# Last stage of a decoder layer: gate and up products with the weights stationary and the tokens moving, the tile loop written out

## The chip, the core and the metric

The kernel runs as one launch on one core of a Trainium2 chip. The metric is the device time of the launch in microseconds. A core has five engines that run their own instruction streams and wait for each other through semaphores: PE (TensorE, matmuls), DVE (VectorE), ACT (ScalarE), POOL (GpSimd) and SP (SyncE, which here issues loads). A PE matmul has a stationary operand, which a weight load (PEld in the profile) puts into the array, and a moving operand that streams through it.

## What is computed

A decoder layer on x of shape 4 x 256 x 256 (1024 tokens of width 256): causal attention with 16 heads, a first gated feed-forward network whose four experts are picked by token id, and a second one whose expert is the best of four by a router. After each part stands x = layernorm(x + part). The change is in the second network. The reference computes it for all experts and selects:

```python
x = tokens of width 256
probs = softmax(x @ Wr + br)
top_w, top_idx = top_k(probs, 1)
g = einsum('td,edf->tef', x, Wg)        # 4 experts, F = 1024
u = einsum('td,edf->tef', x, Wu)
h = silu(g) * u
y = einsum('tef,efd->ted', h, Wd)
out = y[top_idx] * top_w
```

## The kernel before

**Tiles.** The tokens are sorted by expert through a scratch tensor in memory, so that each of NS = 11 tiles of P = 128 tokens needs one expert only (1024 tokens fill 8, and 3 more leave room for the part-filled tiles at the ends of the experts). For each tile the PE computes gate and up (128 tokens x 1024 columns each, contracted over D = 256, NK = 2 steps of 128) and the down product (128 x 256, contracted over F = 1024, NF = 8 steps).

**Three products for one.** Every operand is kept as the sum of two fp16 numbers, hi and lo. A product is hi·hi + hi·lo + lo·hi, so three matmuls (helper `three`, L1286 to L1290). The weights of all experts lie in the tensors wf_hi and wf_lo, EW = 6144 columns an expert, in the order gate, up, down. They are split into hi and lo on the way in: ACT makes hi (`split_hi`, L554), DVE makes lo (`split_lo`, L799), 1024 columns a step. Eight of these steps fall into the last stage: `ENDING` puts 2 ahead of tile 0 and 2 into each of the tiles 0, 1 and 2.

**One tile, before.** PE transposes the tile's tokens (`x_T3`), so that features lie on the partitions; ACT and DVE split the result into a_hi and a_lo (`x_hi3` L736, `x_lo3` L1195). `gate_up` multiplies with a_hi and a_lo **stationary** and 512 weight columns **moving**. It runs in two halves of the F columns, gate and up of a half in two PSUM banks (0, 1 and 2, 3), 12 matmuls a half. ACT applies silu to gate (`silu`, L742), DVE multiplies by up (`gated`, L1202) into hh (128 tokens x 1024, fp32). As tokens lie on the partitions of hh, PE has to transpose it: `h_T3` (L1654), 8 fp32 transposes into the banks 4 and 5. ACT and DVE split the transposed h (`h_hi3` L749, `h_lo3` L1209, 1024 columns each), and `down` multiplies with h stationary and 256 columns of the down weights moving, 24 matmuls into bank 7. Then come residual and layernorm (`statistics`, L1217 to L1223, and `finish`, L1228, on DVE, with two small operations on POOL, L531 and L533, between them), and POOL scatters the rows to the output (L535).

**Order.** Each engine runs the tiles in the order of its code. In tile i PE does gate_up half 0 of tile i, h_T3 of tile i-1, x_T3 of tile i+1, gate_up half 1 of tile i, down of tile i-1. Down of the tiles 0 and 1 is held back until all weights are split (down(0) after tile 2, down(1) within tile 3). Gate_up half 0 of a tile waits until both halves of the tile before are through `gated` (semaphore h3). Four tiles are written out (`PEEL`), six run in a hardware loop of two tiles a turn, and the last stands behind it with a short way out: 8 transposes (L1708), 5 matmuls that only keep the array busy (L1296), and the last down (L1719).

**Addresses.** The expert of a tile is known only at run time. PE loads its number into a register (`expert_of`, TENSOR_LOAD, L1626) and computes the address of each moving weight slice from it. These register operations stand in PE's instruction stream between the matmuls and run on its sequencer: one that makes several sums (FUSED_REGOPS in the profile, ISA in the listings below) and one with a single sum (ALU_OP, or REGISTER_ALU) to every three matmuls.

Of the kernel before, what the change touches and what calls it, by code (L numbers as in the profile page):

```python
# [12 lines left out]
F32, F16, BF16, I32 = mybir.dt.float32, mybir.dt.float16, mybir.dt.bfloat16, mybir.dt.int32  # L13
ALU, ACT, AX = mybir.AluOpType, mybir.ActivationFunctionType, mybir.AxisListType

P = 128
# [34 lines left out]
PEEL = 4  # L51
LOOPS = (NS - 1 - PEEL) // 2
assert PEEL + 2 * LOOPS + 1 == NS
# [8 lines left out]
WARM_START, WARM_GAP, WARM_END = 30, 8, 5  # L62
# [3 lines left out]
def build(nc, x_tok, xT, ids, wqkvT, woT, ctxT, Wr, br, Wf, out):  # L66
    ctx = ExitStack()
    with ctx:
# [7 lines left out]
        wf_hi = sb("wf_hi", [P, E * EW], F16)  # L76
        wf_lo = sb("wf_lo", [P, E * EW], F16)
# [120 lines left out]
        xrow = carve([D], F32)  # L198
# [3 lines left out]
        def h_of(i):  # L202
            return (first_hi[i], first_lo[i]) if isinstance(i, int) and i < 2 else (h_hi, h_lo)
# [3 lines left out]
        def ps16(k, rows=slice(0, P)):  # L207
# [29 lines left out]
        ld3 = [sem(f"ld3_{i}") for i in range(PEEL + 2)]  # L237
# [8 lines left out]
        endT, end_hi, end_lo = sem("endT"), sem("end_hi"), sem("end_lo")  # L246
        a3T, a3hi, a3lo, gu_a, gu_b, sg3, h3, h3T, h3hi, h3lo, y3, r3, bn3, mv3, ve3, xrow_rdy, rs3, f3 = (
            sem(n) for n in ("a3T", "a3hi", "a3lo", "gu_a", "gu_b", "sg3", "h3", "h3T", "h3hi", "h3lo", "y3",
                             "r3", "bn3", "mv3", "ve3", "xrow_rdy", "rs3", "f3"))
# [87 lines left out]
        def _(sp):  # L337
# [64 lines left out]
            for i in range(NS):  # L402
                row = sp.value_load(row_i[0:1, i:i + 1], min_val=0, max_val=NR3 - P)
                if i == 0:
                    sp.wait_ge(scat3, 16 * NS)
                sp.dma_start(XS[:, i, :], sorted3[bass.ds(row, P), :]).then_inc(ld3[min(i, PEEL + 1)], 16)

# [138 lines left out]
        def _(act):  # L546
# [179 lines left out]
            def x_row(i):  # L726

                act.wait_ge(a3T, i)
                a.activation(xrow, XS[:, bass.ds(i, 1), 0:D].rearrange("p o d -> p (o d)"),
                             ACT.Copy).then_inc(xrow_rdy, 1)  # L730

            def x_hi3(i, p):
                act.wait_ge(a3T, i + 1)
                if not (isinstance(i, int) and i < 2):
                    act.wait_ge(gu_b, i - 1)
                a.activation(a_hi[p], ps[:, 6, 0:D].rearrange("p (k t) -> p k t", k=NK), ACT.Copy).then_inc(a3hi, 1)  # L736

            def silu(i, half):
                act.wait_ge((gu_a, gu_b)[half], i + 1)
                if not (isinstance(i, int) and i < 1):  # L740
# [4 lines left out]
            def h_hi3(i):  # L745
                act.wait_ge(h3T, i + 1)
                if not (isinstance(i, int) and i < 3):
                    act.wait_ge(y3, i)
                a.activation(h_of(i)[0], ps[:, 4:6, :].rearrange("p c (k t) -> p (c k) t", t=P),  # L749
                             ACT.Copy).then_inc(h3hi, 1)  # L750

            def tile(i, p, first=False, last=False, splits=((), ())):
                if not isinstance(i, int):
                    x_row(i + 1)
                silu(i, 0)
                if not first:
                    h_hi3(i - 1)
                if not last:
                    x_hi3(i + 1, 1 - p)
                for c in splits[0]:  # L760
                    split_hi(c)
                silu(i, 1)
                for c in splits[1]:
                    split_hi(c)

            x_hi3(0, 0)
# [3 lines left out]
            for i in range(PEEL):  # L770
                splits = ENDING[i + 1] if i + 1 < len(ENDING) else (0, 0)
                tile(i, i % 2, first=i == 0, splits=[range(n, n + splits[0]), range(n + splits[0], n + sum(splits))])
                n += sum(splits)
            assert n == NCH
            act.wait_ge(ld3[PEEL + 1], 16 * (NS - PEEL - 1))
# [983 lines left out]
```

## Time and profile before

| | |
|---|---|
| Runs | 316.97, 317.5 and 321.75 us; median 317.5 us |
| The profiled execution | span 317.3 us |
| PE busy | 249.7 us (79%), 2015 matmuls |
| PE weight loads | 168.8 us (53%) |
| DVE busy | 192.4 us (61%) |
| ACT busy | 134.8 us (42%) |
| POOL busy | 66.7 us (21%) |
| Mean granted TensorE clock | 0.940 |

The last stage, which the change touches, runs from 195.6 us, when the first gate product starts, to the end. A row of the profile gives the source line, the engine, the operation, what it writes and reads, and a count. Busy time of PE is drawn with modelled ends, so the distance between the starts of matmuls says more than their duration: a burst of n equal matmuls that takes t, where one lasts d, has a distance of (t - d)/(n - 1).

### The profile page before, as it was taken

Reading aid. Unit: us, or ns where it says so; the run is one execution under the profiler, and the core shown is the slowest. Engines: PE = TensorE matmul, PEld = TensorE weight load, DVE = VectorE, ACT = ScalarE, POOL = GpSimd, SP = SyncE. Lnnn points to the kernel's source line nnn. Section 1 sums busy time; section 2 is a strip of 40 time slices with the busy share of each in tenths; the row PEclk is TensorE's granted clock in tenths of the full one; section 3 lists DMA queues with packets and bytes.
Section 4 is the critical chain, followed back from the end, with each engine's and each line's share of the span. In section 5 each row is a group of like instructions: output and inputs, shape, how many; then the busy total and the mean of one; then the engine's idle time right before and its main releaser. Section 6 shows DMA issues by size and latency. Waiting matters only on the chain.

```text
span 317.3 us, 5932 instructions
## 1 busy us (share of the span) xinstructions
PE 249.7 (79%) x2015; PEld 168.8 (53%) x2032; DVE 192.4 (61%) x415; ACT 134.8 (42%) x225; POOL 66.7 (21%) x128
## 2 busy tenths in 40 slices
PE   3776589879989775798785566776969999999990
PEld 3454466656756543485665423433745666666570
DVE  4865677777896656868568437566344445545441
ACT  4450555764949744554424332455212312333210
POOL 8400000100140532210113860000203211122222
PEclk9797899999999999979899579999899999999997
DMA  6999045222252445104067123300000000000000
GB/s 213 334 311 276 3 152 181 69 70 66 69 166 69 115 153 153 44 22 135 1 247 284 44 83 89 105 0 0 2 17 20 0 13 17 17 17 17 9 10 6
DMA packets 17416, 28.51 MB, mean 90 GB/s; under 512 B 2733, under 2 KB 12974, under 8 KB 17392
## 3 DMA queue, kind: packets, MB, share of 16 engines
q1 hardware_dynamic: 16048, 25.28, 25.9%
q0 software_dynamic: 1344, 2.90, 2.6%
q8 instruction: 16, 0.26, 0.3%
q14 instruction: 8, 0.07, 0.1%
HBM read 19.43 MB, written 9.50 MB: 91 GB/s over the span
## 4 chain that ended last, share of the span: by engine, by line
PE 56%; DVE 21%; issue 8%; ACT 6%; DMA 3%; POOL 3%; SPq 1%; POOLq 0%; ACTq 0%; DVEq 0%
PE ps L1290 34%; PE ps L1654 3%; DVE arena L965 3%; DVE wf_lo L799 2%; PE ps L1361 2%; PE ps L1400 2%; PE ps L1603 2%; ACT wf_hi L554 2%; PE ps L1548 2%; DVE arena L960 1%; PE ps L1357 1%; DMA ring<-wqkvT 1%; DVE arena L1167 1%; POOL sorted L514 1%; DVE arena L939 1%
## 5 line engine op out<-in xcount | busy, mean ns | idle before, releaser
L1290 PE MATMUL ps<-wf_hi,arena 128*128 x336 | 84.0, 333 | 10.6 <-DVE arena L1202 3.4
L1290 PE MATMUL ps<-wf_lo,arena 128*128 x168 | 55.9, 333 | 0.0
L1290 PEld LDWEIGHTS ps<-wf_hi,arena 128*128 128x128 f16 x336 | 33.4, 99 | 36.1 <-issue 16.1
L742 ACT ACTIVATE arena<-ps 128x512 f32<-128x512 f32 x22 | 13.1, 597 | 68.9 <-PE ps L1290 68.9
L1202 DVE SCALAR_TENSOR_TENSOR arena<-ps,arena 128x512 f32<-128x512 f32 x22 | 15.2, 691 | 22.4 <-PE ps L1654 12.3
L799 DVE SCALAR_TENSOR_TENSOR wf_lo<-ring,wf_hi 128x1024 f16<-128x1024 f32 x17 | 20.6, 1219 | 12.6 <-ACT wf_hi L554 7.5
L1290 PE MATMUL ps<-xT_hi,arena 128*128 (+1 forms) x88 | 21.4, 307 | 1.1 <-DVE arena L1135 1.1
L1290 PEld LDWEIGHTS ps<-wf_lo,arena 128*128 128x128 f16 x168 | 16.7, 99 | 9.4
L531 POOL TENSOR_SCALAR veps<-mv 128x1 f32<-128x1 f32 x11 | 2.5, 225 | 87.3 <-DVE mv L1223 87.3
L965 DVE TENSOR_REDUCE arena<-ps 128x4 f16<-128x1024 f32 x16 | 19.6, 1223 | 1.1 <-PE ps L1361 1.1
L1290 PE MATMUL ps<-arena,xT_hi 128*128 128x512 f16 (+1 forms) x64 | 16.5, 347 | 3.0 <-DVE arena L920 2.1
L554 ACT ACTIVATE wf_hi<-ring 128x1024 f16<-128x1024 f32 x17 | 17.7, 1052 | 0.1
L1217 DVE SCALAR_TENSOR_TENSOR arena<-ps,arena 128x256 f32<-128x256 f32 x11 | 5.3, 483 | 19.6 <-PE ps L1290 17.4
L601 ACT ACTIVATE arena<-ps 128x1024 f32<-128x1024 f32 x16 | 16.5, 1033 | 1.1 <-PE ps L1384 0.7
L960 DVE TENSOR_REDUCE arena<-ps 128x4 f16<-128x512 f32 x16 | 11.0, 689 | 8.6 <-PE ps L1361 8.4
L1357 PE MATMUL ps<-maskS,identB 128*128 128x512 bf16 x27 | 11.0, 408 | 5.1 <-DVE arena L965 3.9
L1361 PE MATMUL ps<-arena 128*128 128x128 f16 x144 | 13.4, 232 | 2.0 <-DVE wf_hi L946 0.9
L535 POOL DMA_INDIRECT out<-arena,out_i x11 | 12.0, 1091 | 13.9 <-DVE arena L1228 13.9
L1400 PE MATMUL ps<-arena 128*32 128x256 f32 (+1 forms) x256 | 13.7, 331 | 1.2 <-ACT arena L607 1.1
L1209 DVE TENSOR_TENSOR arena<-ps,arena 128x1024 f16<-128x1024 f32 x10 | 12.2, 1225 | 3.2 <-ACT arena L749 3.2
L584 ACT ACTIVATE arena<-ps 64x1024 f16<-64x1024 f16 x6 | 6.1, 1018 | 18.1 <-PE ps L1326 18.1
L1548 PE MATMUL ps<-identF,arena 128*128 128x128 f32 x22 | 5.3, 328 | 10.6 <-DVE arena L1172 10.6
(227 smaller groups left out, 534.4 us busy)
## 6 DMA issues: line engine op xcount, KB each, us to landing
ring<-Wf SPq DMA_DIRECT2D x17, 512.0 KB, 3.8
sorted<-fill SPq DMA_DIRECT2D x1, 4515.0 KB, 20.6
arena<-Wf SPq DMA_DIRECT2D x7, 512.0 KB, 8.3
arena<-sorted SPq DMA_DIRECT2D x20, 129.0 KB, 2.2
sorted<-fill SPq DMA_DIRECT2D x1, 1161.0 KB, 6.1
ring<-xT SPq DMA_DIRECT2D x4, 256.0 KB, 5.1
X<-x_tok SPq DMA_DIRECT2D x1, 1024.0 KB, 7.5
ring<-ctxT SPq DMA_DIRECT2D x2, 512.0 KB, 4.1
```

What stands on the lines that cost most here:

```text
L554: a.activation(chunk_dst(ORDER[n], True), src, ACT.Copy, scale=W_SCALE).then_inc(c_hi, 1)
L601: a.activation(Pf[n % 2][:, 1:3], ps[:, 4:6, :], ACT.Exp, scale=DK ** -0.5).then_inc(exped, 1)
L742: a.activation(sg[:, half * 512:(half + 1) * 512], ps[:, 2 * half, :], ACT.Silu, scale=1 / W_SCALE).then_inc(sg3, 1)
L799: v.scalar_tensor_tensor(out=chunk_dst(ORDER[n], False), in0=staged(n)[0], scalar=W_SCALE, in1=chunk_dst(ORDER[n], True), op0=ALU.mult, op ...
L960: v.tensor_reduce(dst[:, 0], ps[:, 0, :].rearrange("p (a k) -> p a k", a=G), AX.X, ALU.max, negate=True).then_inc(maxed, 1)
L965: v.tensor_reduce(dst[:, 1], ps[:, 1:3, :].rearrange("p c (a k) -> p a c k", a=G), AX.XY, ALU.max, negate=True).then_inc(maxed, 1)
L1202: v.scalar_tensor_tensor(out=hh[:, half * 512:(half + 1) * 512], in0=ps[:, 2 * half + 1, :], scalar=inv, in1=sg[:, half * 512:(half + 1) * ...
L1209: v.tensor_tensor(lo, ps[:, 4:6, :].rearrange("p c (k t) -> p (c k) t", t=P), hi, ALU.subtract).then_inc(h3lo, 1)
L1290: last = t.matmul(dst, xs(k), ws(k), start=(k == 0 and m == 0), stop=(k == nk - 1 and m == 2))
L1357: t.matmul(ps[:, bank, :], identB[:, :], maskS[:, :, :].rearrange("p a k -> p (a k)"), start=True, stop=False)
L1361: last = t.matmul(ps[:, bank, i * P:(i + 1) * P], q[:, h, qt * P:(qt + 1) * P], k[:, h // 2, kt * P:(kt + 1) * P], start=not diag, stop=(n ...
L1400: last = t.matmul(ps[i * HEAD:(i + 1) * HEAD, 6, kt * P:S], Vs[:, TB * b + kt, at_:at_ + HEAD], q, start=kt == 0, stop=kt == TB - 1, tile_ ...
```

## The change

The three weight parts change their role only in gate and up. `gate_up` now takes 128 weight columns as the stationary operand and the 128 tokens (a_hi, a_lo) as the moving one. The result has F columns on the partitions and tokens in the free direction, which is what `down` needs, and so the transposes of h (L1654, L1708) and the banks 4 and 5 fall away. A tile's gate and up take 96 matmuls of 128 columns in place of 24 of 512. `h_hi3` and `h_lo3` read hh from SBUF, in two halves of 512 columns. Gate and up of a half signal apart, so silu may start after gate. Gate_up of a half now waits for the same half of the tile before. All eleven tiles are written out, each with its own load semaphore, with the `xrow` copy gone. The expert is loaded a tile ahead, behind `x_T3`, as a byte offset, and the addresses of three hi/lo weight pairs are made together by one register operation ahead of nine matmuls. The `WARM_END` matmuls are gone, `down` waits for r3 (residual read) in place of mv3 and for h3lo in halves.

```diff
-            def h_T3(i):
-                pe.wait_ge(h3, 2 * i + 2)
-                for k in range(NF):
-                    last = t.transpose(ps[:, 4 + k // 4, (k % 4) * P:(k % 4 + 1) * P], hh[:, k * P:(k + 1) * P],
-                                       identF[:, :])
-                last.then_inc(h3T, 1)
             def expert_of(i):
-                return pe.value_load(tile_i[0:1, 1, bass.ds(i, 1)], min_val=0, max_val=E - 1)
+                e = pe.value_load(tile_i[0:1, 1, i:i + 1], min_val=0, max_val=E - 1)
+                return pe.snap(e * (2 * EW))
+            def weights(base, at_, n):
+                cols = bass.ds(base + 2 * at_, 2 * n)
+                return wf_hi8[:, cols].bitcast(F16), wf_lo8[:, cols].bitcast(F16)
+            def addressed(pairs, stationary):
+                for w in pairs:
+                    for half in w:
+                        pe.lower_ap(half, for_matmul_weights=stationary)
-            def gate_up(p, half, expert):
+            def gate_up(i, half, base):
+                p = i % 2
+                if i >= 1:
+                    pe.wait_ge(h3, 2 * i + half - 1)
                 for n in range(2):
-                    at_ = lambda k, n=n: expert * EW + (n * NK + k) * F + half * 512
-                    last = three(ps[:, 2 * half + n, :], lambda k: a_hi[p][:, k], lambda k: a_lo[p][:, k],
-                                 lambda k: wf_hi[:, bass.ds(at_(k), 512)],
-                                 lambda k: wf_lo[:, bass.ds(at_(k), 512)], NK)
-                last.then_inc((gu_a, gu_b)[half], 1)
+                    ws = [weights(base, (n * NK + k) * F + (4 * half + c) * P, P) for c in range(4) for k in range(NK)]
+                    for j, (hi, lo) in enumerate(ws):
+                        c, k = divmod(j, NK)
+                        if j % 3 == 0:
+                            addressed(ws[j:j + 3], True)
+                        dst = ps[:, 2 * half + n, c * P:(c + 1) * P]
+                        t.matmul(dst, hi, a_hi[p][:, k], start=k == 0, stop=False)
+                        t.matmul(dst, hi, a_lo[p][:, k], start=False, stop=False)
+                        last = t.matmul(dst, lo, a_hi[p][:, k], start=False, stop=k == NK - 1)
+                    last.then_inc((gu_a, gu_b)[half], 1)
...
+            for i in range(NS):
+                pe.wait_ge(a3lo, i + 1)
+                gate_up(i, 0, bases[i])
+                if i + 1 < NS:
+                    x_T3(i + 1)
+                    bases.append(expert_of(i + 1))
+                if i == AHEAD3:
+                    down(1, bases[1])
+                gate_up(i, 1, bases[i])
+                if i == 2:
+                    down(0, bases[0])
+                elif i >= 3:
+                    down(i - 1, bases[i - 1])
+            down(NS - 1, bases[NS - 1])
```

ACT's order in a tile becomes silu(i, 0), x_hi3(i+1), split, h_hi3(i, 0), silu(i, 1), split, h_hi3(i, 1); DVE's becomes gated(i, 0), x_lo3(i+1), split, h_lo3(i, 0), gated(i, 1), split, h_lo3(i, 1), then statistics and finish of tile i-1.

The first place is PE in the middle of a tile, from the end of gate_up half 0 to the start of half 1. Before:

```order
L1290 MATMUL ps<-wf_hi,arena 128x512
L1650 REGISTER_ALU
L1654 MATMUL ps<-identF,arena 128x128 [waits h3lo,h3]
L1654 MATMUL ps<-identF,arena 128x128 x7
L1633 REGISTER_ALU
L1638 MATMUL ps<-identF,arena 128x128 [waits a3lo,xrow_rdy]
L1638 MATMUL ps<-identF,arena 128x128
L1290 ISA
L1290 MATMUL ps<-wf_hi,arena 128x512
L1290 REGISTER_ALU
L1290 MATMUL ps<-wf_lo,arena 128x512
```

The same place of the change:

```order
L1634 MATMUL ps<-arena,wf_lo 128x128
L1617 MATMUL ps<-identF,arena 128x128 [waits a3lo,ld3_9]
L1617 MATMUL ps<-identF,arena 128x128
L1599 TENSOR_LOAD tile_i
L1599 ISA x2
L1610 ISA [waits h3]
L1632 MATMUL ps<-arena,wf_hi 128x128
L1633 MATMUL ps<-arena,wf_hi 128x128
L1634 MATMUL ps<-arena,wf_lo 128x128
```

The eight transposes are gone, the load of the next expert has moved in, and one register operation now stands ahead of nine matmuls (the last three rows come three times before the next).

The second place is PE at the end of the program, from the last down but one. Before:

```order
L1290 MATMUL ps<-wf_hi,arena 128x256
L1708 MATMUL ps<-identF,arena 128x128 [waits h3lo,h3]
L1708 MATMUL ps<-identF,arena 128x128 x7
L1296 MATMUL ps<-wf_hi,ones 128x512 [waits a3lo]
L1296 MATMUL ps<-wf_hi,ones 128x512 x4
L1719 ISA [waits end_lo,mv3]
```

And of the change:

```order
L1650 MATMUL ps<-wf_lo,arena 128x256
L1651 MATMUL ps<-wf_hi,arena 128x256
L1610 ISA [waits h3lo,r3]
L1649 MATMUL ps<-wf_hi,arena 128x256
L1650 MATMUL ps<-wf_lo,arena 128x256
```

The last down now follows the one before it with only the wait for r3 and h3lo between them.

The third place is DVE around a tile in the steady part. Before:

```order
L1202 SCALAR_TENSOR_TENSOR arena<-ps,arena 128x512 [waits h3T,sg3]
L1209 TENSOR_TENSOR arena<-ps,arena 128x1024 [waits h3hi]
L1194 REGISTER_ALU
L1195 TENSOR_TENSOR arena<-ps,arena 128x256 [waits a3hi]
L1199 REGISTER_ALU
L1202 SCALAR_TENSOR_TENSOR arena<-ps,arena 128x512 [waits h3T,sg3]
```

And of the change:

```order
L1184 SCALAR_TENSOR_TENSOR arena<-ps,arena 128x512 [waits h3hi,h3lo,gu_a,sg3]
L1175 TENSOR_TENSOR arena<-ps,arena 128x256 [waits a3hi]
L1191 TENSOR_TENSOR arena<-arena 128x512 [waits h3hi]
L1184 SCALAR_TENSOR_TENSOR arena<-ps,arena 128x512 [waits h3hi,h3lo,gu_b,sg3]
L1191 TENSOR_TENSOR arena<-arena 128x512 [waits h3hi]
L1200 SCALAR_TENSOR_TENSOR arena<-ps,arena 128x256 [waits scat_out1,y3]
```

`gated` no longer waits for the transposes (h3T), and the split of h has become two operations of half the size that belong to the same tile.

## Rows read from the trace of the kernel before

**Rows 1.** Chain of work that ended last, tiles 0 to 2; start us, us, what

```profile
195.64 2.76 PE ps L1290 x12
...
198.62 2.60 PE ps L1290 x12
...
202.82 2.76 PE ps L1290 x12
...
219.13 1.24 DVE wf_lo L799
...
220.61 7.04 PE ps L1290 x36
```

**Rows 2.** The same chain, from the down product of tile 2 to the last

```profile
236.69 2.79 PE ps L1290 x24
...
239.69 2.76 PE ps L1290 x12
242.45 0.87 PE ps L1654 x8
...
243.54 5.21 PE ps L1290 x36
...
257.84 0.55 issue
...
286.04 2.76 PE ps L1290 x12
...
303.97 0.87 PE ps L1708 x8
304.84 1.08 PE ps L1296 x5
...
306.07 2.81 PE ps L1719 x24
```

**Rows 3.** Timeline of PE at 89 us; start us, us, engine, line, operation

```profile
89.24 0.61 PE L1361 MATMUL ps<-arena 128*128 128x128 f16 x8
```

**Rows 4.** Source L1361: duration in ns least, median, most; first and last start

```profile
L1361 PE MATMUL ps<-arena x144: 217/219/314, 21.2 to 94.8; 128*128 128x128 f16 x144
```

**Rows 5.** Timeline of PE at 205 us, fp32 transposes

```profile
205.41 1.04 PE L1654 MATMUL ps<-identF,arena 128*128 128x128 f32 x8
```

**Rows 6.** Source L1290, PE's sequencer, 264.6 us to 266.4 us

```profile
L1290 PEldq FUSED_REGOPS  x7: 46/46/46, 264.7 to 266.2; - x7
```

**Rows 7.** Source L1626, the load of the expert's number, 240 us to 290 us

```profile
L1626 PEldq FUSED_REGOPS  x14: 46/151/151, 242.7 to 285.4; - x14
L1626 PEldq TENSOR_LOAD <-tile_i x8: 299/303/312, 242.8 to 285.1; - x8
```

**Rows 8.** Groups by line, 195 to 309 us; busy us, mean ns, idle before

```profile
L1202 DVE SCALAR_TENSOR_TENSOR arena<-ps,arena 128x512 f32<-128x512 f32 x22 | 15.2, 691 | 22.4 <-PE ps L1654 12.3 <-ACT arena L742 10.2
L742 ACT ACTIVATE arena<-ps 128x512 f32<-128x512 f32 x22 | 13.1, 597 | 68.9 <-PE ps L1290 68.9
L1209 DVE TENSOR_TENSOR arena<-ps,arena 128x1024 f16<-128x1024 f32 x10 | 12.2, 1225 | 3.2 <-ACT arena L749 3.2
...
L799 DVE SCALAR_TENSOR_TENSOR wf_lo<-arena,wf_hi 128x1024 f16<-128x1024 f32 x7 | 8.5, 1221 | 0.5 <-ACT wf_hi L554 0.4
...
L1217 DVE SCALAR_TENSOR_TENSOR arena<-ps,arena 128x256 f32<-128x256 f32 x11 | 5.3, 483 | 19.6 <-PE ps L1290 17.4 <-PE ps L1719 2.2
L1195 DVE TENSOR_TENSOR arena<-ps,arena 128x256 f16<-128x256 f32 x11 | 4.6, 415 | 1.0 <-ACT arena L736 1.0
```

**Rows 9.** Stretches: busy of PE, PEld, DVE, ACT, POOL; granted clock; DMA share

```profile
217.50:220.60 3.10, 0.02 (x1) 0.00 (x0) 2.82 (x3) 1.54 (x2) 0.00 (x0) 1.00 0.00 0
220.60:224.00 3.40, 3.39 (x19) 2.48 (x20) 0.00 (x0) 0.00 (x0) 0.00 (x0) 0.60 0.00 0
...
234.00:236.60 2.60, 0.00 (x0) 0.00 (x0) 1.75 (x5) 0.89 (x2) 0.06 (x1) 1.00 0.00 0
...
248.70:267.40 18.70, 18.12 (x117) 11.62 (x116) 9.01 (x18) 5.59 (x10) 3.77 (x6) 1.00 0.04 12
```

More of the change, by code:

```diff
@@ L236, in build @@
         ld2 = [sem(f"ld2_{i}") for i in range(NSA)]
[L237 removed]
+        ld3 = [sem(f"ld3_{i}") for i in range(NS)]
         a2T, a2hi, a2lo, z_rdy, sg2, h2, h2T, h2hi, h2lo, y2, r2, bn2, mv2, rs2, x2_rdy, x2T_rdy, x2T_sb, lg_rdy = (
@@ L743, in silu, with h_hi3 @@
                              scale=1 / W_SCALE).then_inc(sg3, 1)
[L745 to L749, printed above, removed]
-                             ACT.Copy).then_inc(h3hi, 1)
[L752 to L766, printed above, removed]
+            def h_hi3(i, half):
+                act.wait_ge(h3, 2 * i + half + 1)
+                if i >= AHEAD3:
+                    act.wait_ge(y3, i - AHEAD3 + 1)
+                a.activation(h_of(i)[0][:, 4 * half:4 * half + 4],
+                             hh[:, half * 512:(half + 1) * 512].rearrange("p (k t) -> p k t", t=P),
+                             ACT.Copy).then_inc(h3hi, 1)
+            x_hi3(0)
             for _ in range(ENDING[0][0]):
@@ L769, in _ @@
                 n += 1
[L770 removed]
+            for i in range(NS):
                 splits = ENDING[i + 1] if i + 1 < len(ENDING) else (0, 0)
[L772 to L784 removed]
+                silu(i, 0)
+                if i + 1 < NS:
+                    x_hi3(i + 1)
+                for _ in range(splits[0]):
+                    split_hi(n)
+                    n += 1
+                h_hi3(i, 0)
+                silu(i, 1)
+                for _ in range(splits[1]):
+                    split_hi(n)
+                    n += 1
+                h_hi3(i, 1)
+            assert n == NCH
         @block.vector
@@ L1229, in finish, with ending @@
                                 ALU.subtract, ALU.mult).then_inc(f3, 1)
-            def tile(i, p, first=False, last=False, splits=((), ())):
-                gated(i, 0)
-                if not first:
-                    h_lo3(i - 1)
-                if not last:
-                    x_lo3(i + 1, 1 - p)
-                for c in splits[0]:
-                    split_lo(c)
-                gated(i, 1)
-                for c in splits[1]:
-                    split_lo(c)
-            def ending(i, p, scattered=None):
-                statistics(i, p, scattered)
-                finish(i, p)
-            x_lo3(0, 0)
+            def ending(i):
+                statistics(i)
+                finish(i)
+            x_lo3(0)
             for _ in range(ENDING[0][0]):
@@ new lines, in gate_up, with down @@
+                    last.then_inc((gu_a, gu_b)[half], 1)
+            def down(i, base):
+                if i == 0:
+                    pe.wait_ge(c_lo, NCH)
+                else:
+                    pe.wait_ge(r3, i)
+                hs, ls = h_of(i)
+                ws = [weights(base, DOWN + c * D, D) for c in range(NF)]
+                for c, (hi, lo) in enumerate(ws):
+                    if c % 4 == 0:
+                        pe.wait_ge(h3lo, 2 * i + c // 4 + 1)
+                    if c % 3 == 0:
+                        addressed(ws[c:c + 3], False)
+                    t.matmul(ps[:, 7, 0:D], hs[:, c], hi, start=c == 0, stop=False)
+                    t.matmul(ps[:, 7, 0:D], hs[:, c], lo, start=False, stop=False)
+                    last = t.matmul(ps[:, 7, 0:D], ls[:, c], hi, start=False, stop=c == NF - 1)
+                last.then_inc(y3, 1)
```

196 lines of the change are left out of this document (66 added, 130 removed).

## The prediction

> **What bounds the kernel now.** I read the chain of work that ended last first: from 195.64 us on it is almost all PE, one matmul group behind the other [rows 1, 2]. Then the busy time by stretch: in the two steady tiles from 248.7 to 267.4 us PE is busy 18.12 of 18.70 us, DVE 9.01, ACT 5.59, POOL 3.77 [rows 9]. So in the steady part time changes as PE's work changes. Two places wait for others. In tiles 0 to 2 PE stands between tiles, because a half of gate and up waits for both halves of the tile before, and then 3.1 us until the last weights are split (217.5 to 220.6 us, DVE busy 2.82 of it) [rows 1, 9]. Before the down product of tile 2 it stands 2.6 us for DVE [rows 9]. Third, I took the distance of matmul starts, as PE's drawn ends overlap.
>
> **A steady tile.** Five tiles start from 239.69 to 286.04 us, 9.27 us each [rows 2]. Such a tile holds 24 matmuls of 512 columns, 2 x 2.60 = 5.20 us [rows 1]; 8 transposes, 0.87 us; 24 down matmuls, 5.21 - 2.60 = 2.61 us [rows 2]; 2 token transposes at the distance of the fp32 ones, 0.87/8 = 0.11 us, so 0.22 us [rows 2, 5]. That is 8.90 us, and 0.37 us of idle time on average; the largest piece is the 0.55 us at the head of every second tile, where the expert is loaded and the loop turns [rows 2].
>
> The change puts 96 matmuls of 128 columns in place of the 24. No row shows one whose stationary operand is addressed by a register, or six in a row that add into the same 128 columns. The nearest row is the fp16 burst of the attention scores, each matmul with a weight load of its own: (0.61 - 0.219)/7 = 0.0559 us apart [rows 3, 4]. The other end is the fp32 transposes, 0.11 us apart with a weight load each [rows 2, 5]. I take 0.0559, for type, shape and loads are the same, and a matmul moving at a register's address runs today at the same distance as its static neighbours (24 in 2.61 us). Gate and up then cost 96 x 0.0559 = 5.37 us, which is 0.17 more than today; what the tile saves is the transposes and the idle time. New tile: 5.37 + 0.22 + 2.61 = 8.20 us. Five tiles: 5 x (9.27 - 8.20) = **-5.4 us**.
>
> **Addresses.** PE's sequencer today needs 1.5 us for six turns of two register operations and three matmuls, 0.25 us a turn, while the array works [rows 6]. Three matmuls of 128 columns take only 0.17 us, so with today's addresses the sequencer would be the bound, at 0.25/0.17 of the time. With one operation to nine matmuls (0.50 us of array time) I expect it to be hidden, even if the larger one costs a whole turn of 0.25. Loading the expert takes 0.30 and 0.15 us and the steps between, some 0.8 us [rows 7]; it now stands behind the token transposes in mid-tile, where PE has queued matmuls. If they don't cover it, it costs between 0 and the 0.55 us seen today, in ten tiles. I take 0.05 each, **+0.5 us**, for the shorter matmuls drain a queue faster.
>
> **Cover on DVE and ACT.** Per steady tile DVE has 2 gated (0.69), 2 half splits of h (1.225/2 = 0.61 each), the token split (0.42) and the layernorm part; that is as much as now, some 4.5 us in 8.2. ACT reads h in two halves (about the 0.60 us of a 512-column silu each) [rows 8]. Both stay covered. What a half of gate waits for (`gated` of the same half, one tile back) is 5 us old by then.
>
> **The way out.** From the start of tile 9 to the end of the last down it is 286.04 to 308.88 us, 22.84 us [rows 2]. New: tile 9, 8.20; gate and up of tile 10, 5.37; down of tile 9, 2.61; then the bank is read before the last down may write it: end of the last matmul, 0.48 for the residual [rows 8] and 0.24 back to PE (the split ended at 220.37, PE went on at 220.61 [rows 1]), together about 1.0 with the drain; last down 2.81. Sum 19.99, **-2.8 us**. The h split of tile 10 (about 2.2 us with gated) hides under down of tile 9. The transposes (0.87) and the 5 filling matmuls (1.08) went; the wait for the bank is what is late next.
>
> **Tiles 0 to 2.** Today 195.64 to 220.61 us, 24.97 us. PE's own work in the new form is 3 x 5.59 = 16.8 us, but DVE has per tile 2 x 0.69 + 2 x 0.61 + 0.42 + 2 x 1.22 = 5.46 us [rows 8], plus some 0.6 waiting for ACT's hi part of a weight step, less some 0.5 because neighbouring operations overlap: 5.6 us. It starts after the first half (195.64 + 2.68 + 0.2 = 198.5) and its last weight split ends 16.3 us later, as one h split stands behind it: 214.8, down(0) at 215.05. This gain comes from the waits that went: a half waits only for its own half, and gated no longer for transposes that stand behind it in PE's order. **-5.5 us**.
>
> **Tiles 2 to 4.** From down(0) to down(2), 220.61 to 236.69, 16.08 us. In the first 3.40 us the granted clock is 0.60, that is mostly 1.2 in place of 2.4 GHz, after 3.1 us without work [rows 9]; it costs 3.40 x 0.40 = 1.4 us and a little beyond. After the 2.6 us idle at 234 it stayed at 2.4 GHz. New: 2.61 + 2.68 + 0.22 + 2.61 + 2.68 = 10.8 us of work, and a wait of gated 0.69 + hi 0.60 + lo 0.61 + residual 0.48 + 0.24 and hand-overs, 2.8 us: 13.6 us at full clock. The new idle time before down(0) is 2.6 us, between the two cases; I count half of the clock's 1.6: **-1.7 us**. Then down(2) to tile 4: 3.00 us [rows 2] becomes 2.61, **-0.4 us**. Register operations now stand behind waits that are open at down(0), down(2) and the end, +0.1 each: **+0.3 us**.
>
> **Sum.** -5.4 + 0.5 - 2.8 - 5.5 - 1.7 - 0.4 + 0.3 = -15.0 us on the profiled execution's 317.3: 302.3 us; its time is 0.2 below the median of 317.5, so **302.5 us**.
>
> **The rivals.**
>
> *Matmuls of 128 columns further apart (slower).* Place: the 96 matmuls of every tile; mechanism: a weight load at a register's address, or addition into the same columns, that doesn't keep the 0.056 us. Each ns costs 96 x 11 = 1056 ns. From 70 ns on the gain is gone; from 76 ns on the kernel is slower by over 2%; at the 110 ns of the transposes it would stand at 302.5 + 57 = 360 us. For it: no row has this form. Against it: the burst of rows 3. Chance of 76 ns or more 0.10; of 64 to 76 ns (311 to 324 us) 0.09. The Trainium skill, "TensorE: Matmul & The Clock Gate", section "Back-to-back issue gap", gives about 81 ns a matmul for sustained streams of load and 128-column matmul; by it this change would give 302.5 + 26.5 = 329 us. The burst here is only eight long and stands at 56 ns, so the trace disagrees so far.
>
> *The sequencer is the bound in mid-tile.* The load of the expert isn't covered and costs its 0.55 us in ten tiles: +5, 307.5 us. For it: the array drains the queue twice as fast per instruction. Chance 0.12.
>
> *The early tiles give nothing.* Tiles 0 to 2 stay at today's 25 us because the weight steps of ACT and DVE, now with four h operations between them, set the pace otherwise than I counted: 308 us. Chance 0.08.
>
> *As forecast*, 299.5 to 306 us: 0.61 (low end: full clock throughout, no cost of addresses, DVE some 0.3 us faster a tile as its h split reads SBUF).
>
> **Numbers.** The likeliest case gives 302.5. To leave out no more than 2 in 10, the range goes up over the two rivals at 308 to 311: 299.5 to 311. Two per cent, about what a measurement can tell from no change, is 6.35 us: faster means below 311.2. Chances: faster 0.61 + 0.12 + 0.08 = 0.81, within 2% 0.09, slower 0.10.
>
> **What would show it.** In the new profile: starts of gate and up matmuls 56 ns apart; tiles 8.2 us apart from tile 4 on; a half of gate (48 matmuls) 2.7 us; no idle time with "issue" in mid-tile; down(0) near 215 us, down(2) near 229, tile 4 near 231, the last down ending near 293.5. The forecast is wrong if the distance is above 64 ns, if PE idles at the load of the expert, or if DVE is still in tile 2's weight split at 220 us.

## The result, and the profile after

The changed kernel took 301.8 us in the median (300.8 to 303.9); the kernel before, run beside it, 317.2 us. The ratio is 0.952 with a 95% interval of 0.946 to 0.959: faster, by about 15 us. The forecast was 302.5 us. The profiled execution took 303.86 us, its span 301.7.

| Piece of the last stage (us, by starts in the trace) | before | after | difference | forecast |
|---|---|---|---|---|
| start of tile 0's products to down(0) | 24.97 | 19.44 | -5.53 | -5.5 |
| down(0) to down(2) | 16.08 | 13.76 | -2.32 | -1.7 |
| down(2) to tile 4 | 3.00 | 2.63 | -0.37 | -0.4 |
| five steady tiles | 46.35 | 41.16 | -5.19 | -5.4, + 0.25 of the load |
| tile 9 to the end of the last down | 22.84 | 19.9 | -2.94 | -2.8, + 0.25 of the load |
| sum | 113.24 | 96.9 | -16.35 | -15.0 with + 0.3 for registers |

The stage itself began 0.76 us later (196.40 in place of 195.64), which the change did not touch; so the span fell by 15.6.

First view: the costliest groups of the profile (matmuls, then VectorE and ACT). The three matmuls of gate and up, 352 each, stand for the 24 of 512 columns a tile; the columns are line, engine, operation, operands and count, then busy us and mean ns of one, then idle time ahead and who ended it.

```profile
L1632 PE MATMUL ps<-arena,wf_hi 128*128 128x128 f16 x352 | 60.2, 219 | 0.3 <-DVE arena L1175 0.3
...
L1649 PE MATMUL ps<-wf_hi,arena 128*128 x88 | 24.0, 273 | 5.9 <-DVE arena L1200 3.4
...
L1184 DVE SCALAR_TENSOR_TENSOR arena<-ps,arena 128x512 f32<-128x512 f32 x22 | 15.2, 690 | 10.3 <-PE ps L1634 9.5
L742 ACT ACTIVATE arena<-arena 128x512 f16<-128x512 f32 x22 | 13.8, 629 | 16.6 <-DVE arena L1184 16.6
L1191 DVE TENSOR_TENSOR arena<-arena 128x512 f16<-128x512 f32 x22 | 15.2, 690 | 8.8 <-ACT arena L742 8.8
```

The means of the matmuls (219 ns) overlap and say nothing of pace. What does is the distance of starts, in PE's timeline where a down product ends and a half of gate begins:

```profile
248.59 0.27 PE L1651 MATMUL ps<-wf_hi,arena 128*128 x1
248.70 0.22 PE L1632 MATMUL ps<-arena,wf_hi 128*128 128x128 f16 x1
248.75 0.22 PE L1633 MATMUL ps<-arena,wf_hi 128*128 128x128 f16 x1
248.81 0.22 PE L1634 MATMUL ps<-arena,wf_lo 128*128 128x128 f16 x1
248.87 0.22 PE L1632 MATMUL ps<-arena,wf_hi 128*128 128x128 f16 x1
```

The down product's matmuls start 0.11 us apart, those of gate and up 0.05 to 0.06. Over a block of 48 it is 56.1 or 56.2 ns everywhere in the stage, and 96 take 5.39 us. Beside the group read before, [rows 3, 4], that is the same distance.

The waits of PE in the stage (engine and line that waited, whom it waited for, us in all, times, longest):

```profile
PE ps L1649 <- DVE arena L1200: 3.4, 2, 2.7
PE ps L1649 <- DVE wf_lo L779: 2.4, 1, 2.4
PE ps L1617 <- DVE wf_lo L779: 0.8, 1, 0.8
PE ps L1632 <- DVE arena L1175: 0.3, 1, 0.3
```

The last two rows lie ahead of tile 0's products. What is left inside the stage is 2.44 us before down(0), for the last split of weights (L779), and 2.74 and 0.69 us (3.4 in all) before down(2) and the last down, for the residual (L1200) that empties the bank of the down product ahead. Between tiles PE waits for nothing. The stretches answer to [rows 9]; columns are the busy us of PE, PEld, DVE, ACT and POOL, the granted clock, DMA share and GB/s:

```profile
196.40:293.40 97.00, 91.02 (x1340) 87.09 (x1340) 57.88 (x113) 36.72 (x62) 17.88 (x30) 1.00 0.08 24
...
213.20:215.80 2.60, 0.20 (x4) 0.03 (x1) 2.60 (x5) 1.46 (x2) 0.00 (x0) 1.00 0.00 0
215.80:219.20 3.40, 3.36 (x38) 3.10 (x39) 0.96 (x3) 0.00 (x0) 0.00 (x0) 1.00 0.00 0
...
240.40:265.10 24.70, 24.70 (x369) 23.86 (x367) 13.99 (x30) 8.52 (x15) 5.66 (x9) 1.00 0.05 17
```

In the steady part PE is busy 24.70 of 24.70 us, three tiles. The clock stood at its full 2.4 GHz in the whole stage; the 3.40 us at a granted clock of 0.60 behind down(0) [rows 9] did not come again, neither here nor in the second profile of this kernel (run side by side with another at the end of the experiments).

### The profile page after: what moved, and what is told of

It is laid out like the page before. It is cut to its first block, busy times and chain, and to the rows that moved or that the text cites. A ratio compares the mean times of both kernels' runs of the same rounds, so it can differ in the third digit from the quotient of the medians.

```text
span 301.7 us, 7078 instructions
## 1 busy us (share of the span) xinstructions
PE 239.1 (79%) x2714; PEld 192.2 (64%) x2730; DVE 193.3 (64%) x425; ACT 135.8 (45%) x229; POOL 66.8 (22%) x128
## 3 DMA queue, kind: packets, MB, share of 16 engines
q1 hardware_dynamic: 16048, 25.28, 27.8%
## 4 chain that ended last, share of the span: by engine, by line
PE 56%; DVE 21%; issue 8%; ACT 5%; DMA 4%; POOL 3%; SPq 1%; POOLq 0%; ACTq 0%; DVEq 0%
PE ps L1263 8%; PE ps L1632 7%; PE ps L1633 7%; PE ps L1634 7%; PE ps L1649 3%; PE ps L1651 3%; PE ps L1650 3%; PE ps L1334 3%; DVE arena L945 3%; PE ps L1373 2%; DVE wf_lo L779 2%; PE ps L1576 2%; PE ps L1521 2%; PE ps L1330 2%; DVE arena L1147 1%
## 5 line engine op out<-in xcount | busy, mean ns | idle before, releaser
L1632 PE MATMUL ps<-arena,wf_hi 128*128 128x128 f16 x352 | 60.2, 219 | 0.3 <-DVE arena L1175 0.3
L1633 PE MATMUL ps<-arena,wf_hi 128*128 128x128 f16 x352 | 60.3, 218 | 0.0
L1634 PE MATMUL ps<-arena,wf_lo 128*128 128x128 f16 x352 | 60.2, 217 | 0.0
L1633 PEld LDWEIGHTS ps<-arena,wf_hi 128*128 x352 | 34.3, 98 | 0.2
L1632 PEld LDWEIGHTS ps<-arena,wf_hi 128*128 x352 | 33.8, 96 | 0.9 <-issue 0.8
L1634 PEld LDWEIGHTS ps<-arena,wf_lo 128*128 x352 | 33.9, 96 | 0.0
L1649 PE MATMUL ps<-wf_hi,arena 128*128 x88 | 24.0, 273 | 5.9 <-DVE arena L1200 3.4
L779 DVE SCALAR_TENSOR_TENSOR wf_lo<-ring,wf_hi 128x1024 f16<-128x1024 f32 x17 | 20.6, 1220 | 12.5 <-ACT wf_hi L552 7.4
L1650 PE MATMUL ps<-wf_lo,arena 128*128 x88 | 24.0, 273 | 0.0
L1651 PE MATMUL ps<-wf_hi,arena 128*128 x88 | 24.0, 273 | 0.0
L1263 PE MATMUL ps<-xT_hi,arena 128*128 (+1 forms) x88 | 23.1, 325 | 1.1 <-DVE arena L1115 1.1
L742 ACT ACTIVATE arena<-arena 128x512 f16<-128x512 f32 x22 | 13.8, 629 | 16.6 <-DVE arena L1184 16.6
L1191 DVE TENSOR_TENSOR arena<-arena 128x512 f16<-128x512 f32 x22 | 15.2, 690 | 8.8 <-ACT arena L742 8.8
```

The costliest lines, as they stand in the source:

```text
L779: v.scalar_tensor_tensor(out=chunk_dst(ORDER[n], False), in0=staged(n)[0], scalar=W_SCALE, in1=chunk_dst(ORDER[n], True), op0=ALU.mult, op ...
L1263: last = t.matmul(dst, xs(k), ws(k), start=(k == 0 and m == 0), stop=(k == nk - 1 and m == 2))
L1632: t.matmul(dst, hi, a_hi[p][:, k], start=k == 0, stop=False)
L1633: t.matmul(dst, hi, a_lo[p][:, k], start=False, stop=False)
L1634: last = t.matmul(dst, lo, a_hi[p][:, k], start=False, stop=k == NK - 1)
L1649: t.matmul(ps[:, 7, 0:D], hs[:, c], hi, start=c == 0, stop=False)
```

## The experiments

Every kernel was timed beside the kernel before on its chip; ratios are to it. The medians of the kernel before were 317.2 us beside the changed kernel and 320.0, 320.3 and 321.0 beside the three groups of experiments, so a difference of 1% between times of different groups says little, and the ratios and the length of the stage are what is compared. The last stage starts between 193.5 and 198.3 us from one profile to the next; its length is taken from the start of its first gate matmul to the start of its last down matmul, 96.6 us in the changed kernel and 113.0 in the kernel before (0.3 less than by the end).

### Do the grouped addresses matter? One sum ahead of each weight

The addresses are no longer made in groups; each is summed where its matmul uses it.

```diff
-                        if j % 3 == 0:
-                            addressed(ws[j:j + 3], True)
```

> The changed kernel, with the addresses of gate and up no longer made in groups: two single register sums stand among every three matmuls (693 ALU operations more, 88 grouped ones fewer). Theory (the sequencer needs about 0.11 us for each register operation between matmuls and would be the bound at 0.22 us a turn against 0.17 us of array time): from the end of a down product on, some 26 of the 32 turns of a tile run at 0.22 us and the load of the expert adds 0.8, so a steady tile takes about 9.2 us in place of 8.23, gate and up matmuls stand 65 to 75 ns apart on average, and the kernel takes 8 to 12 us more than the change, 310 to 314 us. Rival (the array alone sets the pace and the grouping is worth nothing): 56 ns apart, within 1 us of the change, 301.8 us.

Measured: 324.6 us, ratio 1.017 (1.009 to 1.026): all of the gain is gone, and more. The size was missed by over 10 us. PE's timeline inside a half, with the starts in the first column:

```profile
247.15 0.22 PE L1630 MATMUL ps<-arena,wf_hi 128*128 128x128 f16 x1
247.21 0.22 PE L1631 MATMUL ps<-arena,wf_hi 128*128 128x128 f16 x1
247.26 0.22 PE L1632 MATMUL ps<-arena,wf_lo 128*128 128x128 f16 x1
247.38 0.22 PE L1630 MATMUL ps<-arena,wf_hi 128*128 128x128 f16 x1
```

The starts within three are 0.05 to 0.06 us apart, and 0.11 to 0.12 lie before the next three. Of every three matmuls two have a single sum on PE's sequencer ahead of them. A sum takes 32 ns, but one begins 0.112 us after the other at the least, so three matmuls take 0.23 to 0.24 us: about 80 ns each (78 to 82 from block to block) where the array needs 56. The half behind a down product still ran at 56 ns. The sequencer had run ahead while the down matmuls took 109 ns each: the sums for the half that starts at 252.32 us were made from 250.49 on. Together a steady tile takes 9.97 us (8.23 with groups; 9.2 expected). The expectation counted the loss of steady tiles alone. Tiles 0 to 2 have no down products to run ahead under, so all of their halves went at 80 ns (down(0) came 27.8 us after the start, not 19.4), and the clock fell behind down(0). Of the 22.0 us that the stage grew, 8.4 lie before down(0), 8.7 in the five steady tiles and 1.7 in this fall of the clock. The load of the expert was not covered here either: at eight places behind the token transposes PE stood up to 0.4 us, 2.5 in all. The stretch with the fall:

```profile
220.00:224.00 4.00, 1.90 (x24) 1.58 (x24) 2.90 (x5) 2.04 (x3) 0.00 (x0) 1.00 0.00 0
224.00:228.00 4.00, 4.00 (x24) 2.94 (x23) 0.21 (x1) 0.00 (x0) 0.00 (x0) 0.57 0.02 4
```

So in this form the sequencer is the bound in most of the stage, and what the new products gain depends on fewer register operations between them.

### How much grouping is enough? One operation for each pair

```diff
-                        if j % 3 == 0:
-                            addressed(ws[j:j + 3], True)
+                        addressed(ws[j:j + 1], True)
```

> The changed kernel, with one register operation of two sums ahead of each three gate and up matmuls instead of one of six sums ahead of nine. Theory (one operation and its step cost about 0.13 us, below the 0.17 us of three matmuls): matmuls stay 56 ns apart, within 1 us of the change, 301.8 us. Rival (groups must be large): the turn is longer than 0.17 us, each tile grows by 1 us or more, above 310 us.

Measured: 303.4 us, ratio 0.952 (0.943 to 0.960); stage 96.6 us as in the changed kernel, every block at 56.1 to 56.3 ns. All register rows of the line that makes the addresses, of the changed kernel and then of this one (engine queue, operation, count, then least, median and most ns):

```profile
L1610 PEldq FUSED_REGOPS  x165: 60/74/83, 196.2 to 290.7; - x165
L1610 PEldq ALU_OP  x11: 32/32/32, 196.3 to 279.9; - x11
```

```profile
L1610 PEldq FUSED_REGOPS  x385: 37/37/88, 197.0 to 291.4; - x193
```

Two sums in one operation (37 ns) cost hardly more than one (32); six cost 74. Where the sequencer ran ahead of the array, the operations with two sums began 0.115 us apart (0.112 for single sums), so with two sums it is the step that costs and not the sums; one such step fits under the 0.17 us of three matmuls, and two single ones (0.22) do not. One operation for three matmuls is enough; the group of three pairs is not needed for the time.

### Do registers cost anything at all? A fixed expert

All addresses become constants and no register sum is left between the matmuls (the load of the expert's number stays, unused); every tile uses the weights of expert 0, so the output is not the layer's.

```diff
-                cols = bass.ds(base + 2 * at_, 2 * n)
+                cols = slice(2 * at_, 2 * at_ + 2 * n)
...
-                for w in pairs:
-                    for half in w:
-                        pe.lower_ap(half, for_matmul_weights=stationary)
+                return
```

> The changed kernel, with the weights of expert 0 for all tiles in the last stage: weight addresses are constants, no register stands in a matmul or weight load and the register sums are gone (the output is that of expert 0; the load of the number stays). Theory (a weight load at a register's address costs what a constant one costs, and the sums are hidden): 56 ns apart as in the change, tiles of 8.2 us, within 1 us of 301.8 us. Rival (registers cost part of the 56 ns or of the tile's 0.02 us of idle time): faster by more than 2 us.

Measured: 302.9 us, ratio 0.952 (0.943 to 0.961), stage 96.3 us, 0.3 less. The waits before down(0), down(2) and the last down are 2.32, 2.62 and 0.58 in place of 2.44, 2.74 and 0.69, and the blocks keep 56 ns. Register addresses cost about 0.1 us at each of these three places, where a wait is open ahead of them, and nothing elsewhere.

### Was the load of the expert covered? Back to the tile's head

```diff
+                if i >= 1:
+                    bases.append(expert_of(i))
                 gate_up(i, 0, bases[i])
                 if i + 1 < NS:
                     x_T3(i + 1)
-                    bases.append(expert_of(i + 1))
```

> The changed kernel, with the expert of a tile loaded at the head of the tile, right before its first gate product, instead of in the middle of the tile before. Theory (the load takes about 0.8 us of the sequencer, the queued down matmuls cover it, and the 0.55 us idle at every second tile of the kernel before came from the loop's turn and its waits): tiles stay at 8.2 us, within 1 us of 301.8 us. Rival (the 0.55 us was the load): idle time of 0.3 to 0.55 us at each tile's head, 3 to 6 us slower, 305 to 308 us.

Measured: 304.0 us, ratio 0.952 (0.946 to 0.958), stage 96.6 us with no idle time at any head. The load takes the same as before the change, 0.30 and 0.15 us:

```profile
L1599 PEldq TENSOR_LOAD <-tile_i x11: 295/302/308, 185.8 to 280.0; - x11
L1599 PEldq FUSED_REGOPS  x11: 151/151/151, 186.2 to 280.4; - x11
```

With 24 down matmuls ahead of it the sequencer has its work done before PE needs it. So the 0.55 us that stood at the head of every second tile [rows 2] were not the load as such. What else the old head held is the loop's turn and register sums that need the number of the tile ([rows 7] has 14 operations to 8 loads, this kernel 11 to 11); which of the two cost the time was not tried.

### Where do tiles 0 to 2 gain? The wait for both halves, put back

```diff
-                    pe.wait_ge(h3, 2 * i + half - 1)
+                    pe.wait_ge(h3, 2 * i)
```

> The changed kernel, with the old wait put back: half 0 of gate and up waits until both halves of the tile before are through the gating. Theory (this wait is what the changed kernel got rid of in tiles 0 to 2): PE stands 1.5 us ahead of tile 1 and of tile 2, down of tile 0 starts 3.0 us later than in the change (near 218.9 us), steady tiles stay at 8.23 us as the wait is 5 us old there; 3 us slower, 304.8 us. Rival (DVE's and ACT's weight splits set the pace of tiles 0 to 2 whatever PE waits for): PE stands there but down of tile 0 starts within 0.5 us of the change; 301.8 us.

Measured: 305.7 us, ratio 0.958 (0.952 to 0.963); the stage took 100.0 us, 3.4 more. The chain of work that ended last (start us, us, what) now leaves PE at each of tiles 1 and 2:

```profile
198.90 0.95 ACT wf_hi L552
199.88 1.22 DVE wf_lo L779
201.10 0.13 DVE arena L1191
201.24 0.39 issue
201.63 0.69 DVE arena L1184
202.32 0.45 issue
202.77 0.22 PE ps L1632
```

PE waits 1.60 us there, and 1.51 at tile 2. Still, down(0) waited 2.44 us as before, and came 22.86 us after the start, 3.4 later: the later PE ended, the later the last split of weights ended. Were the sum of VectorE's work the bound, down(0) would have come within 0.5 us of its old place, as the rival has it.

### The same question from the other side: eight transposes a tile

Eight fp32 transposes into unused banks after the first half of tiles 1 to 10, as the kernel before had.

```diff
+                for k in range(NF if i else 0):
+                    t.transpose(ps[:, 4 + k // 4, (k % 4) * P:(k % 4 + 1) * P], identF[:, :], identF[:, :])
```

> The changed kernel, with 8 fp32 transposes of the identity into the free banks 4 and 5 put back where the old ones stood in the tiles 1 to 10; nothing reads or waits for them. Theory (PE's time is the tile's time from tile 3 on, and tiles 0 to 2 are paced by DVE): 0.87 us more in each of the tiles 3 to 10, together 7.0 us, and the two in tiles 1 and 2 are hidden in the 2.6 us that PE stands before down of tile 0: 308.8 us. Rival (PE paces tiles 1 and 2 too): 8.7 us, 310.5 us. Rival (PE is not the bound): under 3 us.

Measured: 314.4 us (311.7 to 317.8), ratio 0.984 (0.975 to 0.994). In the profile, of the shortest execution (311.7), the eight cost their full 0.875 us a tile, in tiles 1 and 2 too:

```profile
202.65 0.88 PE ps L1668 x8
203.53 0.22 PE ps L1617 x2
209.14 0.88 PE ps L1668 x8
```

down(0) came 21.19 us after the start (19.44 + 2 x 0.875 = 21.19), after the same 2.44 us. So tiles 0 to 2 go at PE's pace, and the expectation, which hid two of the ten under VectorE's work, is wrong there. The stage took 107.0 us, 10.4 more. Ten times 0.875 is 8.75 of it; the other 1.7 are 3.4 us at half clock that began at 216.6, 1.2 us after down(0):

```profile
216.60:220.00 3.40, 3.40 (x22) 2.59 (x20) 0.42 (x1) 0.00 (x0) 0.00 (x0) 0.50 0.00 0
```

### The wait alone, in the kernel before

The kernel before with nothing but the finer wait.

```diff
-                    pe.wait_ge(h3, 2 * i)
+                    pe.wait_ge(h3, 2 * i - 1)
```

> The kernel before with one edit: its first half of a tile waits only for the transposed tokens of its own first half, as the changed kernel does; all else (products of 512 columns, transposes, loop, single sums) stays. It asks how much of the gain of tiles 0 to 2 is owed to the wait alone. Theory: in the form before, TensorE stood still for 1.6 and 1.8 us ahead of tiles 1 and 2; the finer wait lets the first half's products start under VectorE's layernorm of the second half, so most of that goes, 2 to 3.4 us in the last stage (113.2 to about 110.5), a total near 315 us against the 317 to 320 of the kernel before. Rival: the product's transposes and the copies after them keep VectorE as busy as before, so the wait only moves to the second half or to the first down product, and the last stage changes by under 1 us.

Measured: 316.9 us against 321.0 of the kernel before in the same rounds, ratio 0.980 (0.970 to 0.991). The chain before tile 1 and tile 2 is unbroken PE now (compare [rows 1]):

```profile
200.34 5.18 PE ps L1290 x24
...
206.61 5.33 PE ps L1290 x24
...
234.49 0.24 issue
234.72 7.05 PE ps L1290 x36
```

From the start to down(0) it took 21.35 us, 3.6 less than before. That is 3.6 of the 5.5 us that these tiles gained; the rest is two times eight transposes (1.75) and what else differs. In the profile the stage as a whole (110.5 us) gained only 2.5, since the clock fell a second time, behind down(2) (36 matmuls in 7.05 us, 5.21 in [rows 2]):

```profile
218.70:222.10 3.40, 3.39 (x17) 2.49 (x18) 0.00 (x0) 0.00 (x0) 0.00 (x0) 0.51 0.02 5
232.00:234.70 2.70, 0.00 (x0) 0.00 (x0) 1.75 (x5) 0.90 (x2) 0.13 (x1) 1.00 0.00 0
235.70:239.10 3.40, 3.40 (x18) 2.42 (x17) 0.20 (x1) 0.00 (x0) 1.09 (x1) 0.50 0.11 39
```

This profile is of the longest of four executions (318.3 us; the shortest took 312.5), so the 3.6 us before down(0), where the clock was full, can be relied on, and whether the second fall belongs to this kernel can't be told.

### What is left: a second bank for the down product

Down products go to two banks in turn, so one need not wait until the residual has emptied the other's.

```diff
...
-                else:
-                    pe.wait_ge(r3, i)
+                elif i >= 2:
+                    pe.wait_ge(r3, i - 1)
+                out_bank = 7 - 3 * (i % 2)
...
```

The down matmuls then write this bank in place of bank 7, and the residual reads it.

> The changed kernel, with the down products of even and odd tiles in two PSUM banks (7 and 4), so that down waits for the residual read of two tiles back. Theory (the 2.9 us before down of tile 2 and the 0.9 us before the last down are waits for that read of bank 7): both vanish, 3.7 us faster than the change, 298.1 us. Rival (PE's time saved before down of tile 2 is given back as a later wait for DVE, which still has to do the work of tiles 1 and 2): under 1.5 us faster.

Measured: 298.9 us (297.5 to 305.1), ratio 0.935 (0.929 to 0.941). The waits before down(2) and the last down are gone, the one before down(0) stands at 2.44; the stage takes 92.8 us, 3.8 less. Behind the last product 0.7 us come back: the layernorm and scatter of tile 9 are still on VectorE and GpSimd when tile 10's are due.

### And the first down product half a tile later

In addition down(0) moves behind the first half of tile 3, and down(1), down(2) and down(3) with it, so that gate and up products stand in PE's order while VectorE ends the weights. VectorE's layernorms of tiles 0 to 3 move with them, two a tile.

```diff
...
-                if i == AHEAD3:
-                    down(1, bases[1])
+                if i in (3, 4):
+                    down(2 * i - 6, bases[2 * i - 6])
                 gate_up(i, 1, bases[i])
-                if i == 2:
-                    down(0, bases[0])
-                elif i >= 3:
+                if i in (3, 4):
+                    down(2 * i - 5, bases[2 * i - 5])
+                elif i >= 5:
                     down(i - 1, bases[i - 1])
```

> As the run with two banks, and down of tile 0 no longer stands after tile 2 but after the first half of tile 3, so that gate and up of tile 3 fill the wait for the last weight split; downs of the tiles 0 to 3 come two a tile in the tiles 3 and 4. Theory: the 2.4 us that PE stands before down of tile 0 vanish as well, 6.4 us faster than the change in all, 295.4 us. Rival (DVE, with the layernorms of four tiles in two, becomes late): PE waits 1 to 3 us in tile 4 or 5 and the time is 297 to 299 us.

Measured: 298.4 us, ratio 0.934 (0.929 to 0.939). The stage takes 90.2 us, 6.4 less, and PE never stands in it:

```profile
196.80:287.10 90.30, 90.29 (x1340) 87.16 (x1340) 56.74 (x112) 36.38 (x62) 17.79 (x29) 1.00 0.09 26
```

The stage did what was expected, but the total lay only 0.5 us under the kernel with two banks. To see where it went, it and the changed kernel were run side by side once more.

> The changed kernel as it is, on the same chip and in the same rounds as the next run and the kernel before: 300 to 304 us, ratio 0.947 to 0.957; last stage 96.4 to 96.9 us.

> The changed kernel with the down products on two banks of PSUM and the first down product after the first half of tile 3, as before, now on the same chip and in the same rounds as the changed kernel. Theory: the last stage is shorter by 6.4 us (90.2 to 90.6 against 96.6 to 96.9), and 0.7 us come back behind the last product, so the total lies 5 to 6 us under that of the changed kernel beside it (295 to 298). Rival: VectorE and ScalarE, which now have no slack in tiles 0 to 2, give part of it back, and the total lies only 3 to 4 us under it.

Measured: 302.7 us (ratio 0.947, 0.939 to 0.955) and 298.6 us (0.930, 0.923 to 0.937): 4.2 us apart, nearer to the rival. The two stretches of the stage, of the changed kernel and then of the other:

```profile
194.40:291.40 97.00, 91.01 (x1340) 87.07 (x1340) 57.86 (x113) 36.77 (x62) 17.85 (x30) 1.00 0.08 24
```

```profile
198.20:288.70 90.50, 90.43 (x1340) 87.15 (x1340) 56.88 (x112) 36.44 (x62) 17.78 (x29) 1.00 0.09 26
```

By its starts the stage is 6.4 us shorter (90.2 and 96.6) and the part behind it 0.7 longer, as the theory had it, and PE does not wait in it, so the rival's cause is not there. But the stage begins at 198.27 us in place of 194.44, and this takes 3.8 us of it back in the profiled spans (299.8 and 297.9). Up to the stage the mean granted clock is 0.94 in the one and 0.90 in the other, and the edit lies behind all of that work. Such starts differ without this edit too: the other profile of this version began the stage at 196.81 us, and those of the versions with down(0) at its old place between 193.49 and 197.10. Over the whole executions (span times one less the mean granted clock) the ten of this version lost 20.7 us of clock on average, the eight of the changed kernel 17.5; in the profiles about 1 of these 3 lies behind the last product, where no matmul is left. So of the 5.7 us that the stage and the part behind it give (6.4 less 0.7), 4.2 arrive in the medians, with a lower clock outside the stage; whether the version causes that is open.

## Why the prediction was right

**The distance of 56 ns** carried it, and stood: 1056 pairs of weight load and matmul, addressed by registers, six in a row into the same 128 columns, kept the distance of the burst of eight [rows 3, 4]. Neither the address nor the addition into the same columns costs time. The Trainium skill, "TensorE: Matmul & The Clock Gate", section "Back-to-back issue gap", gives about 81 ns for a sustained stream of such pairs; this case's trace disagrees, with 56.1 to 56.2 ns in every block of the stage. Only the kernel with one sum ahead of each weight ran at about 80 ns, and there its sequencer's steps account for it.

**A steady tile** was forecast at 8.20 us plus 0.05 for the load, and took 8.23. The transposes' 0.87 and 0.37 of idle time less 0.19 for the longer products make 1.05 of the 1.04 measured.

**Addresses and the load**: covered, as forecast. An operation for six sums was bounded at a turn of 0.25 us and lasted 0.07. The allowance of 0.5 us for the load was not needed; the 0.3 for register operations behind open waits is what the fixed expert took off the stage. The rival that the sequencer becomes the bound is wrong for the kernel as changed and right without grouping: a turn of two sums took 0.23 to 0.24 us, near the 0.25 that the prediction had read, and the kernel was slower than the one before (ratio 1.017).

**The way out** was -2.8 and measured -2.94. The wait that was to be late next is there: 0.69 us before the last down, of which the residual is 0.49.

**Tiles 0 to 2**: -5.5 forecast, -5.53 measured, by a step that is partly wrong. "DVE has per tile ... 5.6 us" was taken as the pace. VectorE was busy 17.3 of 19.4 us, so the sum of its work was about right, yet PE ran through its products without a gap, and both experiments (a late PE, a longer PE) moved down(0) by their full size. ACT and VectorE wait for PE in each of these tiles, at the transposes of the next tile's tokens, and only behind the last of them does a chain of theirs run without waiting for PE. ACT's and VectorE's rows from there on:

```profile
210.75 0.39 ACT L728 ACTIVATE arena<-ps 128x256 f16<-128x256 f32 x1 [0.67 <-PE ps L1617]
211.03 1.05 ACT L552 ACTIVATE wf_hi<-arena 128x1024 f16<-128x1024 f32 x1
212.11 1.23 DVE L779 SCALAR_TENSOR_TENSOR wf_lo<-arena,wf_hi 128x1024 f16<-128x1024 f32 x1 [0.51 <-ACT wf_hi L552]
213.25 0.68 DVE L1191 TENSOR_TENSOR arena<-arena 128x512 f16<-128x512 f32 x1
213.85 0.68 DVE L1184 SCALAR_TENSOR_TENSOR arena<-ps,arena 128x512 f32<-128x512 f32 x1
214.45 1.21 DVE L779 SCALAR_TENSOR_TENSOR wf_lo<-arena,wf_hi 128x1024 f16<-128x1024 f32 x1
```

These are the split of the tokens and one of weights on ACT, then on VectorE that split's other half, h_lo, `gated` and the last weight split. PE's last product ended at 213.40, while VectorE was at h_lo, so `gated` did not wait for it. From the end of the transposes (210.71) to down(0) it is 5.13 us here and 5.13 to 5.14 in the kernels with the late PE, the longer PE and two banks. With one sum ahead of each weight the last product ended so late that `gated` did wait for it, and down(0) came 2.10 us behind it. So down(0) is fixed by PE up to these transposes and by ACT and VectorE behind them. The two counts, 5.59 us a tile for PE and 5.6 for VectorE, were too near to be told apart by arithmetic, and the total came out right by either; that part of the hit is luck. That the gain comes "from the waits that went" holds: the finer wait alone brought 3.6 us to the kernel before, and the old wait put back cost the changed kernel 3.4.

**Down(0) to down(2)** was mis-sized: 13.76 us, as worked out at full clock (13.6), but only half of the clock's 1.6 us was counted as gained, and all of it was. With that and the allowance for the load that was not needed (0.5) the forecast of -15.0 for the stage becomes -16.3; it measured -16.35.

**The frame of the sum.** The text set the span of 317.3 us beside the median of 317.5 as if it were the execution's time. A time lies some 2 us above its span (303.86 and 301.7 after). The span of 302.3 us that the sum gives came out as 301.7: 1.35 us more were gained in the stage and 0.76 lost by its later start. The median lies 2.1 us under the profiled execution, and this happens to cancel the 2 us between span and time, which is luck; by the steps alone the forecast of the profiled execution would have been 304.5 us (302.3 + 2.16), measured 303.86.

**The early tiles give nothing**, the third rival, is excluded by the table.

## What to carry to other kernels

A product whose result is wanted transposed can be computed transposed, if its narrower matmuls run at the distance that a burst of the same type and shape shows in the kernel's own trace; read the distance of starts, not the mean duration. Halving the columns of a matmul halves the time that the sequencer has for it: count the steps between matmuls (here 0.11 us each with one sum or two in it), and put sums together until one step covers more array time than it takes. And read what PE waits for after the change: here 3.4 of the 5.9 us of waits that were left went with a second bank of PSUM, in an edit of seven lines.

## What the runs showed of the hardware

- A register operation between matmuls costs its engine's queue a place more than a duration: single sums of 32 ns began 0.112 us apart at the least, operations with two sums (37 ns) 0.115 us; one with six sums lasted 74 ns.
- The sequencer's lead is used up over tens of matmuls: behind a down product (24 matmuls, 109 ns each) one whole half of 48 ran at 56 ns although the sequencer's own pace for it was about 80 ns a matmul.
- The clock did not follow the length of the idle time alone. After 2.44 us of idle before down(0) it stayed full in both profiles of the changed kernel and in the kernels with the late PE, the load at the head and two banks, and fell in the one with transposes; it fell after 2.10 us with one sum ahead of each weight. After 2.7 us before down(2) it stayed full in the changed kernel and in the kernel before, and fell in the kernel before with the finer wait. Each fall cost 1.4 to 1.8 us. What else decides stays open. The kernel that never lets PE stand in this stage showed no fall there in two profiles.
- The split of h from SBUF to SBUF (690 ns for an instruction of 512 columns) was no faster than from PSUM (1225 ns for one of 1024, 612 for each 512, [rows 8]), and a part of this may be that it is two instructions in place of one; the low end of the range had counted on the opposite.
